# Gated cross-attention with a linear layer: the block-diagonal spread made by eight masked products on VectorE and ScalarE instead of two broadcast products on VectorE and GpSimd

## The reference, cut to what matters

```python
Q = (q @ Wq.T + bq).reshape(bs, sl, 16, 32)      # q = layernorm(x), x is [4, 512, 512]
K = (k @ Wk.T + bk).reshape(bs, sl, 16, 32)      # k = v = ctx, [4, 512, 512]
V = (v @ Wv.T + bv).reshape(bs, sl, 16, 32)
score = einsum('bshd,bsgd->bshg', Q, K)          # per token: 16 heads against 16 heads
weight = softmax(score, axis=-1)
attn = einsum('bshg,bsgd->bshd', weight, V).reshape(bs, sl, 512)
x = x + tanh(g_xattn[0]) * (attn @ Wo.T + bo)
x = x + tanh(g_ffn[0]) * (layernorm(x) @ (weight_f * scale[:, None]).T + bias)
```

## Time and profile before

| | |
|---|---|
| median of 3 runs | 323.98 us (323.53 to 325.38) |
| the profiled execution | 322.51 us, its span 320.8 us |
| TensorE matmul busy | 292.4 us, 91% of the span |
| VectorE busy | 216.5 us, 67% |
| ScalarE busy | 141.3 us, 44% |
| GpSimd busy | 107.3 us, 33% |
| spread on VectorE, 8 instructions | 32.4 us |
| spread on GpSimd, 8 instructions | 26.2 us |
| mean granted TensorE clock | 0.968 |

### The profile page before, as it was taken

How to read it: one execution, slowest core, us unless ns; L and a number is a source line. 1 busy time by engine, 2 the same in 40 slices (tenths; PEclk the granted TensorE clock), 3 DMA queues, 4 the chain that set the end, 5 groups by cost and what they waited for, 6 DMA issues and landing times.

```text
span 320.8 us, 6628 instructions
## 1 busy us (share of the span) xinstructions
PE 292.4 (91%) x2562; PEld 258.9 (81%) x2562; DVE 216.5 (67%) x321; ACT 141.3 (44%) x277; POOL 107.3 (33%) x83
## 2 busy tenths in 40 slices
PE   6499699759998999999999999999999997894895
PEld 6498699548986899889988898889988996774684
DVE  3857479835876696568774887568746953497463
ACT  4355424572377033923385236803592239304500
POOL 3500215520445133533173126214433342042422
PEclk9869899959999999999999999999999999799999
DMA  7966688473543735364543556184436226512001
GB/s 224 332 225 212 218 227 264 137 190 85 188 151 118 191 133 195 115 149 140 176 142 135 127 196 190 71 196 153 174 131 134 66 87 183 127 66 67 33 33 67
DMA packets 64596, 48.52 MB, mean 151 GB/s; under 512 B 35776, under 2 KB 53952, under 8 KB 64576
## 3 DMA queue, kind: packets, MB, share of 16 engines
q1 hardware_dynamic: 64576, 48.25, 49.0%
HBM read 31.46 MB, written 16.78 MB: 150 GB/s over the span
## 4 chain that ended last, share of the span: by engine, by line
PE 61%; DMA 13%; DVE 10%; SPq 8%; issue 4%; ACT 3%; POOL 1%; DVEq 0%; POOLq 0%
PE acc L377 48%; PE score_ps L463 6%; DMA k_scratch<-k_t 6%; PE turn_ps L406 4%; DMA q_scratch<-q_t 3%; PE attn_ps L478 3%; DVE spread L786 3%; SPq L230 2%; DMA x_norm<-x 2%; DMA q_pad<-q_scratch 2%; ACT late L602 2%; SPq L271 2%; DVE x_norm L711 2%; DVE stats L689 2%; SPq L256 1%
## 5 line engine op out<-in xcount | busy, mean ns | idle before, releaser
L602 ACT ACTIVATE late<-attn_ps 32x256 f32<-32x256 f32 x128 | 48.1, 376 | 24.9 <-PE attn_ps L478 18.2
L946 POOL TENSOR_TENSOR spread<-probs_t,same_token 128x1536 f32<-128x1536 f32 (+1 forms) x8 | 26.2, 3278 | 75.2 <-DVE probs_t L778 75.2
L377 PEld LDWEIGHTS acc<-ctx_parts,wk_parts 128*128 128x128 f32 x384 | 48.9, 199 | 1.9 <-issue 1.4
L377 PE MATMUL acc<-ctx_parts,wk_parts 128*128 128x256 f32 x384 | 49.6, 290 | 0.8 <-DVE wk_parts L675 0.8
L377 PE MATMUL acc<-wf_parts,x_parts 128*128 128x512 f32 (+1 forms) x192 | 44.7, 387 | 3.0 <-ACT x_parts L541 1.6
L377 PE MATMUL acc<-xa_parts,wq_parts 128*128 128x256 f32 x384 | 47.4, 283 | 0.0
L377 PE MATMUL acc<-wo_parts,xa_parts 128*128 128x512 f32 x192 | 46.1, 395 | 0.8 <-ACT xa_parts L541 0.8
L377 PEld LDWEIGHTS acc<-xa_parts,wq_parts 128*128 128x128 f32 x384 | 46.7, 192 | 0.0
L377 PE MATMUL acc<-wv_parts,ctx_parts 128*128 128x512 f32 x192 | 45.7, 393 | 0.0
L377 PEld LDWEIGHTS acc<-wo_parts,xa_parts 128*128 128x128 f32 x192 | 35.7, 189 | 10.2 <-issue 1.7
L377 PEld LDWEIGHTS acc<-wf_parts,x_parts 128*128 128x128 f32 x192 | 34.7, 188 | 11.1 <-ACT x_parts L541 2.4
(11 more groups left out here) (62 smaller groups left out, 352.9 us busy)
## 6 DMA issues: line engine op xcount, KB each, us to landing
ctx_raw<-ctx_t SPq DMA_DIRECT2D x8, 512.0 KB, 4.4
x_norm<-x SPq DMA_DIRECT2D x8, 512.0 KB, 6.0
k_scratch<-k_t SPq DMA_DIRECT2D x8, 512.0 KB, 3.5
k_rows<-k_scratch SPq DMA_DIRECT2D x32, 128.0 KB, 2.9
q_scratch<-q_t SPq DMA_DIRECT2D x8, 512.0 KB, 3.4
q_pad<-q_scratch SPq DMA_DIRECT2D x32, 128.0 KB, 2.8
v_scratch<-v_or_norm SPq DMA_DIRECT2D x8, 512.0 KB, 2.8
v_keys<-v_scratch SPq DMA_DIRECT2D x8, 512.0 KB, 4.8
```

Of the source, the lines that this page charges most:

```text
L377: last = pe.matmul(dst, left(a, k), right(b, k), start=(n == 0), stop=(n == len(terms) - 1))
L602: nc.scalar.activation(attn_t[HD * q:HD * (q + 1), :, GT * t:GT * (t + 1)] .rearrange("p m (o e) -> p m o e", e=OCT), attn_ps[HD * t:HD * ...
L946: nc.gpsimd.tensor_tensor(spread[:, first:].rearrange("p o h t -> p (o h) t"), probs_t[:, first:].rearrange("p o h -> p (o h)").unsqueeze( ...
```

## The change

The spread is made by 8 products, one for each token `e` of an oct: `spread[:, :, :, e] = probs_t * same_token[:, e]`, where the mask column is a per-partition scalar. Each product reads the 512 elements of `probs_t` contiguously and writes 512 elements that lie 8 elements (32 bytes) apart. ScalarE makes tokens 0 to 3 (`spread_first`, now there), VectorE tokens 4 to 7 (`spread_last`, now there), and GpSimd none. On ScalarE the four products stand behind `exp(i)` and `x1_high(i+1)` and ahead of `k_bias(i+1)`. `attend` waits for both parts before its first matmul.

```diff
-POOL_OCTS = 6
-LAST_POOL_OCTS = 8
+ACT_TOKENS = OCT // 2
...
-                for b, spread_done in enumerate((spread_dve, spread_pool)):
-                    pe.wait_ge(spread_done, c + 1)
+                pe.wait_ge(spread_dve, c + 1)
+                pe.wait_ge(spread_act, c + 1)
+                for b in range(2):
...
+            def spread_first(c):
+                act.wait_ge(s_back, c + 1)
+                reached(act, attn_mm, 2 * c)
+                if first(c):
+                    act.wait_ge(w_lo, pieces_to(WO, 1))
+                    act.wait_ge(consts_made, 2)
+                for e in range(ACT_TOKENS):
+                    last = nc.scalar.activation(spread[:, :, :, e], probs_t[:], ACT.Identity,
+                                                scale=same_token[:, e:e + 1])
+                last.then_inc(spread_act, 1)
...
                 if exists(i):
                     exp(i)
+                if exists(i + 1) and not first(i):
+                    x1_high(i + 1)
+                if exists(i):
+                    spread_first(i)
                 if exists(i + 1):
-                    if not first(i):
-                        x1_high(i + 1)
                     k_bias(i + 1)
...
-            def spread_first(c):
+            def spread_last(c):
 
                 dve.wait_ge(s_back, c + 1)
                 reached(dve, attn_mm, 2 * c)
-                n = OCTS - pool_octs(c)
-                nc.vector.tensor_tensor(
-                    spread[:, :n].rearrange("p o h t -> p (o h) t"),
-                    probs_t[:, :n].rearrange("p o h -> p (o h)").unsqueeze(2).broadcast_to([P, n * HT, OCT]),
-                    same_token[:].unsqueeze(1).broadcast_to([P, n * HT, OCT]), ALU.mult).then_inc(spread_dve, 1)
+                for e in range(ACT_TOKENS, OCT):
+                    last = nc.vector.tensor_scalar(spread[:, :, :, e], probs_t[:], same_token[:, e:e + 1], None, ALU.mult)
+                last.then_inc(spread_dve, 1)
...
-            pool.wait_ge(w_lo, pieces_to(WO, 1))
-            pool.wait_ge(consts_made, 2)
 
             def pool_step(i):
-                if exists(i):
-                    spread_last(i)
```

More of the change, by code:

```diff
@@ L156, in gated_attention_kernel @@
             sem(n) for n in ("s_turned", "s_peak", "s_sub", "s_exp", "s_total", "s_inv", "s_probs", "s_back"))
-        spread_dve, spread_pool = sem("spread_dve"), sem("spread_pool")
+        spread_dve, spread_act = sem("spread_dve"), sem("spread_act")
         n_stats = [sem(f"n{i}_stats") for i in (1, 2)]
@@ L215, in final @@
             return isinstance(c, int) and c == CHUNKS - 1
-        def pool_octs(c):
-            return LAST_POOL_OCTS if final(c) else POOL_OCTS
         def late_f(c):
@@ L849, in vector_step @@
                     turned_lo(xa_parts, x1_hi, x1_lo, i + 1)
-                spread_first(i)
+                spread_last(i)
                 if first(i):
@@ L940, in x2_bias @@
                                             ).then_inc(x2_biased, 1)
[L942 to L951, removed]
             made = sem("made")
```

## The result

| | median | ratio to the kernel before (95% interval) |
|---|---|---|
| before | 324.68 us | |
| changed | 332.08 us (330.65 to 332.62, 4 runs) | 1.0247 (1.0194 to 1.0301) |

The change costs 2.5%, 8.0 us. The ratio goes by fast runs alone: it leaves out one slow run of the kernel before (327.33 us), which the median of 324.68 counts, and so gives 8.0 us where the medians differ by 7.4. The profiled execution took 330.65 us with a span of 328.9, against 322.51 and 320.8. So 8.1 us are to be found in the trace.

The account below looks back on a forecast made before the run. It took TensorE to bound the steady chunks and the spread the last one. Chunk 0 +3.9, chunk 1 +2.9, chunks 2 to 6 +3.0, last chunk -0.8 make 9.0 us: 324.0 + 9.0 = 333.0, range 324.1 to 337.

Parts of the forecast that it names:

- The place: In front of the query layer, whose first half needs the bank k_bias empties; steady chunks have 1.8 us of slack.
- ScalarE's product: ScalarE's four scattered-write products take 4.2 us, priced from lay_keys' scattered read; bounds 2.3 and 5 us.
- VectorE's product: VectorE's four products take 4.6 us, hidden in a steady chunk by its 0.65 us of idle.
- Chunk 0: +3.9 us: query layer idles 4.75 us, the clock costs 1.5, and lay_keys releases score(1) 3.9 later.
- Chunk 1: +2.9 us: query layer idles 2.7, the clock costs 1.5, and the 1.34 us wait for the values goes.
- Chunks 2 to 6: +3.0 us: k_bias ends at 154.1 against 153.49, so 0.6 us in each of five chunks, paid in full.
- The last chunk: -0.8 us: the spread is the bound there, attend starts 0.8 earlier, and the rest follows.
- The clock: TensorE falls to half speed after 2.55 us of idle, costing 1.5 us in chunk 0 and in chunk 1.
- The second rival: Free scattered write, and the clock holds through 2.85 us of idle in chunk 0: sum -1.5, 322.4 us; chance 0.10.
- the first rival: Free scattered write (products 2.3 us), and the clock falls in chunk 0: sum +0.1, 324.1 us; chance 0.12.

Follow-up runs that it names:

- k_first: The changed kernel with ScalarE's four products moved behind the four instructions of k_bias (in step 0 also behind the tanh); 321.19 us, ratio 0.9939.
- contig: The changed kernel with all eight products writing contiguously into a token-major buffer, so the attention sums are wrong; 325.38 us, ratio 1.0074.
- k_first0: The changed kernel with ScalarE's products moved behind k_bias and the tanh in step 0 alone; 326.93 us, ratio 1.0136.
- act3: The changed kernel with 3 of the 8 products on ScalarE and 5 on VectorE; 326.39 us, ratio 1.0044.

## Why the prediction was right

The forecast was 333.0 us and +9.0; measured are 332.1 and +8.0. By its steps:

- **The place.** The wait of the query layer for `k_bias` is what the change makes, in all seven chunks where it was put. This is shown by k_first, which removes it by order alone, and by the runs with 2, 3, 4 and 6 products.
- **ScalarE's product.** Forecast 4.2 us for four, from a scattered read. Measured 4.15 to 4.35. The row of the nearest stride priced a write it had never been measured on: 1.03 ns more per element against 0.93 from the read. That a write costs ScalarE what a read does was an assumption of the prediction, and it held. So did the 0.1 us for the mask operand (717 ns in `contig` against 622 for the plain copy of the earlier trace rows). The page "SBUF — State Buffer" of the Trainium skill, in its note on cachelines, says that each access that crosses to a new line pays a penalty. The trace agrees for this write, 1242 against 717 ns; that the line is the reason is not shown, since no run has another step.
- **VectorE's product.** Mis-sized: forecast 4.6 us for four, measured 2.2 to 2.3. The scattered write costs it 230 ns in 512 elements, not the 530 that the prediction added. The estimate of 1.4 us a product, which the prediction worked out from the Trainium skill ("Vector Engine (DVE) Microarchitecture Reference", section 5.2), is twice the 0.71 us of this case; the page's 2.50 ns a column were measured with a step of 24 words and two sources, and here the step is 8 words and the source one. The error cost little, since VectorE was hidden everywhere but in the last chunk.
- **Chunk 0.** Forecast +3.9, found +3.7 (3.4 by the marks and 3.6 by the ratios in k_first0). The idle was right, 4.44 us for 4.75, and so was the order of the chain behind it: `lay_keys` ended at 72.05 and released score(1). That the sum fits so well is partly luck. The clock loss was sized too small, 2.4 us and not 1.5 (a query layer of 8.31, not 7.35). Against it score(0) ran at full clock in the changed kernel's trace and at half in the one before, so that `probs_t` was ready 1.0 us sooner behind it (7.97 against 9.01 us), which no step of the prediction has.
- **Chunk 1.** +2.9 as forecast: 2.49 idle and 1.5 for the clock, 1.34 returned, and 0.3 more in the output layer behind score(1), where the clock came back later (6.29 against 5.99 us).
- **Chunks 2 to 6.** Forecast 0.6 each, found 0.47. ScalarE's neighbouring instructions overlap by 0.1 us (high part and products) and 0.25 us (products and `k_bias`), which the sum left out.
- **The last chunk.** Here steps were off and nearly cancel, which is luck. `attend` lost its whole wait, 1.53 and not 0.8, because VectorE was cheap. And 1.3 were given back behind it: the prediction said that the rest follows, and had no term for the wait for ScalarE's copies, which grows from 1.65 to 2.85 us, nor for the clock behind it. Whether the longer wait or the execution made the clock fall is open, as said above. In the profiled execution score(7) ran at full clock (2.50 us against 3.47), which is the remaining -1.0 and no effect of the change: behind the same wait of 3.1 us it took 3.2 to 3.6 us in seven of twelve traces and 2.5 in five, in either order of ScalarE's work. Without it the last chunk would be at -0.3, where -0.8 had been forecast. The prediction also read that GpSimd and VectorE ran one after the other there. No row says so, and their records overlap (284.03 to 287.76 and 284.50 to 289.90 us), but VectorE's 2048 elements took 5.40 us there, and its 2560 in chunk 0 took 2.83.
- **The clock.** The prediction took one row, 2.55 us of idle and then half speed, as if it were a bound. In the two places where it was used the clock did fall, in chunk 1 behind 2.49 us, a little under that bound. As a rule it does not hold: see below. The second rival had 0.10 for a clock that holds through 2.85 us; `act3` shows that it can, through 2.94. (A slip in the first rival: by its own chain score(1) comes at 70.05, not 70.15, so its sum is near 0 and not +0.1.)

What stays open is when the clock falls behind a wait of 1.6 to 3 us. The wait's length does not decide it, and no run here shows what does.

## What to carry to other kernels

An engine at 44% has room only where nobody waits for what stands behind the new work. The same four products cost 10 us more ahead of the instructions that empty a matmul bank than right behind them, so look at what is queued behind, and who waits for that. Price a scattered access from the nearest scattered row of the same engine, not from the contiguous ones: for ScalarE a read gave the price of a write to about a tenth, while for VectorE, which had no such row, the guess was twice too dear. When a wait on TensorE goes or moves, look at the next idle behind it and at the matmuls that follow: in the tail a fallen clock cost 1.6 us, as much as the earlier `attend` had gained, and eight more small matmuls got it back.

## What the runs showed of the hardware that was not expected

- Behind waits of the same length TensorE's clock fell in one trace and held in another. Ahead of the query layer it fell behind 2.14, 2.48, 2.49, 2.51 and 2.95 us, and held behind 2.14, 2.31, 2.71 and 2.94. Ahead of the `f` layer in the tail it fell behind 1.64 and 1.74 and held behind 1.65. Behind the wait of 3.1 us ahead of score(7) it fell in seven of twelve traces. A fall cost a query layer 1.4 to 1.6 us, and 2.3 to 2.4 behind waits of 4.4 us and more; it cost score(7) 0.7 to 1.1.
- A write with a step of 32 bytes costs ScalarE 1.03 ns more per element (1242 against 717 ns for 512) and VectorE's `tensor_scalar` 0.45 (708 against 478).
- TensorE pays for a scattered moving operand: a step of 512 elements from one element to the next takes 64 matmuls from 1.95 to 3.70 us.
- score(0) started anywhere from 36.3 to 40.1 us in the profiled executions, before any work that the edits touch. Single profiles are best compared from a mark behind it.
